# Routing and row scatter of a mixture of experts, moved into the last sections of the transformer before it

## The reference

```python
def _moe(x, rw, rb, w1, b1, w2, b2):          # E = 8 experts, K = 2 chosen, FF = 1024
    xf = x.reshape(T, D)                       # T = 4096, D = 256
    router_weights = jax.nn.softmax(xf @ rw + rb, axis=-1)
    topw, topi = jax.lax.top_k(router_weights, K)
    topw = jax.nn.softmax(topw, axis=-1)
    combine = zeros((T, E)).at[arange(T)[:, None], topi].add(topw)
    h = gelu(einsum('td,edf->etf', xf, w1) + b1[:, None, :])
    eo = einsum('etf,efd->etd', h, w2) + b2[:, None, :]
    return einsum('etd,te->td', eo, combine)
...
x = _layernorm(x + _attn(x, encoder_output, ...), ln2_g, ln2_b)
x = _layernorm(x + _moe(x, router_w, router_b, e_w1, e_b1, e_w2, e_b2), ln3_g, ln3_b)
```

## Time and profile before

| What | Value |
|---|---|
| median of 3 runs | 3463.55 us |
| the profiled execution: its time, its span | 3469.08 us, 3466.9 us |
| PE busy over the span | 2949.5 us (85%) |
| DVE, ACT, POOL busy | 2096.4, 1958.2, 1631.2 us |
| end of the last POOL step of the transformer | 2699.7 us |
| first matmul of the first expert block | 2858.9 us |
| first load of the final section | 3379.3 us |

### The profile page before, as it was taken

The page is one execution under the profiler, slowest core; times in us unless marked ns, Lnnn a source line. Parts: engine busy times, 40 slices in busy tenths (PEclk is TensorE's granted clock), DMA queues, the critical chain, the costliest instruction groups (busy, mean ns, idle before and its releaser), DMA issues. The chain is left out here.

```text
span 3466.9 us, 58062 instructions
## 1 busy us (share of the span) xinstructions
PE 2949.5 (85%) x19009; PEld 1713.3 (49%) x19009; DVE 2096.4 (60%) x4293; ACT 1958.2 (56%) x4164; POOL 1631.2 (47%) x2833
## 2 busy tenths in 40 slices
PE   6889999888989999998988999989888409999990
PEld 3435444543544354445435443544342409999980
DVE  4877796787879678877867796785435200000007
ACT  4675767576756757675766667573534104444431
POOL 4655563673657357546836572664230171111114
PEclk9999999999999999999999999988898559999995
DMA  3004230523144042214213241413330258999974
GB/s 89 16 22 101 58 85 23 123 59 71 53 81 74 28 86 59 55 31 95 54 42 67 57 74 31 86 36 78 58 51 14 79 195 269 326 324 326 324 255 145
DMA packets 309028, 355.41 MB, mean 103 GB/s; under 512 B 33534, under 2 KB 286334, under 8 KB 308656
## 3 DMA queue, kind: packets, MB, share of 16 engines
q1 hardware_dynamic: 300576, 335.27, 37.0%
q0 software_dynamic: 6480, 17.05, 1.3%
q10 hardware_dynamic: 1728, 0.01, 0.0%
HBM read 291.86 MB, written 61.11 MB: 102 GB/s over the span
## 5 line engine op out<-in xcount | busy, mean ns | idle before, releaser
L1254 ACT ACTIVATE probs<-ps,nbias,sc 128x512 f32<-128x512 f32 x1024 | 790.3, 778 | 278.3 <-DVE nbias L1135 219.9
L1001 POOL TENSOR_SCALAR pq<-probs,rstep 128x512 f16<-128x512 f32 x1024 | 713.5, 697 | 251.6 <-PE ps L1368 168.2
L1152 DVE TENSOR_REDUCE m<-ps 128x1 f32<-128x512 f32 (+3 forms) x1024 | 560.6, 582 | 292.8 <-PE ps L1394 150.0
L1132 DVE TENSOR_REDUCE nmax<-ps 128x2 f32<-128x1024 f32 x512 | 620.4, 1212 | 95.9 <-PE ps L1360 95.2
L1391 PE MATMUL ps<-kst,qst 96*128 96x512 bf16 (+3 forms) x1024 | 331.0, 355 | 89.6 <-issue 50.7
L1144 DVE TENSOR_SCALAR big<-ps 128x1024 bf16<-128x1024 f16 x512 | 347.9, 679 | 62.4 <-PE ps L1368 61.0
L1368 PE MATMUL ps<-id,pq 128*128 128x128 f16 x4096 | 331.0, 226 | 47.5 <-DVE big L1144 41.2
L1785 ACT ACTIVATE hT<-moe_ps,e_b 128x128 f32<-128x128 f32 x568 | 208.1, 367 | 280.8 <-PE moe_ps L1728 242.0
L1413 PE MATMUL ps<-qst,kst 108*128 108x512 bf16 (+3 forms) x1024 | 306.1, 353 | 65.0 <-ACT big L1273 29.6
L1368 PEld LDWEIGHTS ps<-id,pq 128*128 128x128 f16 x4096 | 262.0, 101 | 191.4 <-issue 126.2
L1273 ACT ACTIVATE big<-ps 128x512 f32<-128x512 f32 (+3 forms) x640 | 274.1, 480 | 142.0 <-PE ps L1416 96.6
(11 more groups left out here) (202 smaller groups left out, 4609.8 us busy)
## 6 DMA issues: line engine op xcount, KB each, us to landing
e_w<-in_L_xattn_e_w_dram SPq DMA_DIRECT2D x142, 1024.0 KB
wring<-in_L_xattn_ff_w_dram SPq DMA_DIRECT2D x96, 256.0 KB, 2.9
parts<-parts_sb SPq DMA_DIRECT2D x64, 384.0 KB, 3.1
kst<-parts SPq DMA_DIRECT2D x192, 128.0 KB, 4.8
qst<-parts SPq DMA_DIRECT2D x192, 128.0 KB, 5.0
moe_in<-rows_in SPq DMA_DIRECT2D x71, 132.0 KB
rows_in<-zero SPq DMA_DIRECT2D x17, 528.0 KB, 4.1
xn<-in_ctx_dram SPq DMA_DIRECT2D x16, 512.0 KB, 3.9
```

Of the source, the lines that this page charges most:

```text
L1001: nc.gpsimd.tensor_scalar(pq[:, u % 2, h, :], probs[:, u % 2, h, :], rstep[:, u % 2, h:h + 1], HALF_ROUND, ALU.mult, ALU.add).then_inc(SIG ...
L1132: nc.vector.tensor_reduce(nmax[:, n % 2, :], ps[:, a:a + 2, :], AX.X, ALU.max, negate=True).then_inc(SIG["M"], 1)
L1152: nc.vector.tensor_reduce(m32[:, g % 2, t, h:h + 1], bank(("A", B, s, n))[:, 0:width], AX.X, ALU.max, negate=True).then_inc(SIG["am"], 1)
L1254: nc.scalar.activation(probs[:, u % 2, h, :], ps[:, BANKS[("S", B, s, u)][h], :], ACT.Exp, bias=nbias[:, u % 2, h:h + 1], scale=sc[:, s:s ...
```

## The change

The routing and the scatter are done per batch, as steps of the transformer's list: rT and dr (transpose and copy), rL (logits), rl, rx, rm, ry, ri (softmax, two best, weights and choice), rP and rp (places of the rows), and sc (8 indirect DMAs of a batch on POOL). The batches are routed in the order 4, 5, 0, 1, 2, 3, 6, 7. The first may not begin before the exact stage (6, 3). Batches 4 to 7 are still in X, which has 4 places now; batches 0 to 3 are read back from `mid` (step LR on SP) into the places of batches 4 and 5. The weight ring has 6 pieces for 8.

Each expert has a region of 33 blocks in `rows_in`, so a row's place follows from a running count for each expert, and the number of an expert's rows need not be known ahead. A row carries 3 x 8 words behind its 256 features: for each expert where the result goes, its weight, and whether it is the token's first choice. The filling with zero rows is gone: one block of pad rows is written at the start, and after the last routing SP copies it behind the last row of each expert, at the place that the count says (8 copies DRAM to DRAM).

In the experts' part the routing, the loading of `mid` and the scatter are gone. DVE makes the block plan from the counts alone (9 steps for the owners, 8 more for the places of the blocks). SP loads the weights of slot 0 first, then the 4 blocks, then the weights of the slots 1 to 3, and reads a block's place before its load. DVE finishes a part at the end of a block: it multiplies the output and its bias by the weight and adds x for the first choice (4 instructions in place of 2). In the final section DVE adds the two parts in one instruction of 128x1024, adds eps and negates the mean; the shift goes to POOL. A load of the parts of batch c + 4 waits for the output of batch c, where it waited for the sums of batch c.

```diff
-ROW = D + NE
+ROW = D + 3 * NE
 TOKENS = NBATCH * N
+REGION = TOKENS // BLOCK + 1
+NOWHERE = NE * REGION
+ALL_BLOCKS = NOWHERE + 1
+X_DEEP = 4
+ROUTED = (4, 5, 0, 1, 2, 3, 6, 7)
+AGAIN = {0: 0, 1: 1, 2: 0, 3: 1}
+ROUTED_LAST = ROUTED[-1]
...
+    return AGAIN[B] if B in AGAIN else B % X_DEEP
...
-RING = 8
+RING = 6
...
-        step("LX", B, 0, 0, ("ST", B - 3, 5, 0) if B >= 3 else None)
+        step("LX", B, 0, 0, ("ST", B - X_DEEP, 5, 0) if B >= X_DEEP else None)
...
         norm(B, 5)
-        step("ST", B, 5, 0, ("gb", B, 5, NT - 1))
+        last = routed_before(B)
+        if B in AGAIN:
+            step("LR", B, 6, 0, ("ST", B, 5, 0), ("sc", place_taken(B)[-1], 6, 2 * NT - 1))
+        for m in range(KT):
+            step("rT", B, 6, m, ("LR", B, 6, 0) if B in AGAIN else ("gb", B, 5, NT - 1), ROUTING_OPENS if B == ROUTED[0] else ("rL", last, 6, 0))
+            step("dr", B, 6, m, ("rT", B, 6, m))
+        step("rL", B, 6, 0, ("dr", B, 6, KT - 1), last is not None and ("rp", last, 6, 0))
+        step("rl", B, 6, 0, ("rL", B, 6, 0))
+        step("rx", B, 6, 0, ("rl", B, 6, 0))
+        step("rm", B, 6, 0, ("rx", B, 6, 0))
+        step("ry", B, 6, 0, ("rm", B, 6, 0))
+        step("ri", B, 6, 0, ("ry", B, 6, 0))
+        step("rP", B, 6, 0, ("ri", B, 6, 0))
+        step("rp", B, 6, 0, ("rP", B, 6, 0))
+        for n in range(2 * NT):
+            step("sc", B, 6, n, ("rp", B, 6, 0))
+        if B in AGAIN:
+            step("ST", B, 5, 0, ("gb", B, 5, NT - 1))
...
+                if kind == "LR":
+                    sp.wait_ge(s_stored, 16 * B + 16)
+                    sp.wait_ge(s_sc[place_of(B)], 16 * 2 * NT * len(place_taken(B)))
+                    sp.dma_start(X[:, place_of(B), :, 0:D], mid[B].rearrange("(t p) d -> p t d", p=P)).then_inc(s_again[place_of(B)], 16)
...
-                    fill_some_rows()
...
+            after(sp, "rp", ROUTED_LAST, 6)
+            for e in range(NE):
+                if e == 0:
+                    sp.wait_ge(s_zeroed, 16)
+                end = sp.value_load(run_int[0:1, e:e + 1], min_val=0, max_val=NOWHERE * BLOCK - BLOCK)
+                sp.dma_start(every_row[bass.ds(end, BLOCK), :], every_row[NOWHERE * BLOCK:ALL_BLOCKS * BLOCK, :]).then_inc(s_zeroed, 16)
+            sp.wait_ge(s_stored, 16 * len(AGAIN))
+            sp.wait_ge(s_zeroed, 16 * (NE + 1))
+            for place in range(X_DEEP):
+                sp.wait_ge(s_sc[place], 16 * 2 * NT * len([b for b in ROUTED if place_of(b) == place]))
...
+                if kind == "sc":
+                    k, t = n // NT, n % NT
+                    after(pool, "rp", B, s)
+                    nc.gpsimd.indirect_dma_start(rows_in.rearrange("b r d -> (b r) d"),
+                                                 bass.IndirectOffsetOnAxis(ap=slot_of[:, B, k, t:t + 1], axis=0),
+                                                 X[:, place_of(B), t, :], None).then_inc(s_sc[place_of(B)], 16)
...
+                if kind == "ri":
+                    dve.wait_ge(s_route, 6)
+                    for t in range(NT):
+                        last = nc.vector.max_index(idx[:, t, :], top[:, t, :], pr[:, t, :])
+                    then(last, 1)
+                    then(nc.vector.tensor_copy(idf[:, :, :], idx[:, :, 0:2]), 2)
+                    after(dve, "ry", B, s)
...
+                    then(nc.vector.tensor_copy(X[:, place_of(B), :, :].bitcast(U32)[:, :, D:D + NE], goes_to[:, :, :]), 9)
+                    for k in range(2):
+                        last = nc.vector.tensor_tensor(at_pos[:, k, :, :], eq[:, k, :, :], wide(wt[:, k, :]), ALU.mult)
+                    then(last, 10)
+                    then(nc.vector.tensor_tensor(X[:, place_of(B), :, D + NE:D + 2 * NE], at_pos[:, 0, :, :], at_pos[:, 1, :, :], ALU.add), 11)
+                    then(nc.vector.tensor_copy(X[:, place_of(B), :, D + 2 * NE:ROW], eq[:, 0, :, :]), 12)
...
+                if kind == "rp":
+                    after(dve, "rP", B, s)
+                    filled = bank(("rP", B, s, 0))
+                    then(nc.vector.tensor_tensor(pos[:, :, :], filled[:, 0:NT * NE].rearrange("p (t e) -> p t e", e=NE),
+                                                 every_tile(run[:, :]), ALU.add), 1)
+                    then(nc.vector.tensor_tensor(run[:, :], filled[:, NT * NE:(NT + 1) * NE], run[:, :], ALU.add), 2)
+                    for k in range(2):
+                        last = nc.vector.tensor_tensor(at_pos[:, k, :, :], eq[:, k, :, :], pos[:, :, :], ALU.mult)
+                    then(last, 3)
+                    then(nc.vector.tensor_reduce(slot_f[:, :, :], at_pos[:, :, :, :], AX.X, ALU.add), 4)
+                    then(nc.vector.tensor_copy(slot_of[:, B, :, :], slot_f[:, :, :]), 5)
+                    then(nc.vector.tensor_copy(run_int[:, :], run[:, :]), 6)
...
+                if kind == "rL":
+                    after(pe, "dr", B, s, KT - 1)
+                    rest_loaded(pe)
+                    bank_free(pe, e)
+                    for t in range(NT):
+                        for k in range(KT):
+                            last = nc.tensor.matmul(bank(e)[:, t * NE:(t + 1) * NE], rT[:, k, t * P:(t + 1) * P], rw[:, k, :],
+                                                    start=(k == 0), stop=(k == KT - 1))
+                    last.then_inc(SIG["rL"], 1)
+                if kind == "rP":
+                    after(pe, "ri", B, s)
+                    bank_free(pe, e)
+                    flat = chosen[:, :, :].rearrange("p t e -> p (t e)")
+                    nc.tensor.matmul(bank(e)[:, 0:NT * NE], earlier[:, :], flat, start=True, stop=False)
+                    for t in range(1, NT):
+                        nc.tensor.matmul(bank(e)[:, t * NE:NT * NE], ones[:, :], flat[:, 0:(NT - t) * NE], start=False, stop=(t == NT - 1))
+                    for t in range(NT):
+                        last = nc.tensor.matmul(bank(e)[:, NT * NE:(NT + 1) * NE], ones[:, :], flat[:, t * NE:(t + 1) * NE],
+                                                start=(t == 0), stop=(t == NT - 1))
+                    last.then_inc(SIG["rP"], 1)
...
             sp.wait_ge(s_r, OWNERS_READY)
-            for slot in range(WSLOTS):
-                load_weights(slot, slot)
-            sp.wait_ge(s_sc, 16 * 2 * NTILES)
+            load_weights(0, 0)
+            sp.wait_ge(s_r, PLACES_READY)
             for slot in range(WSLOTS):
                 load_block(slot, slot)
+            for slot in range(1, WSLOTS):
+                load_weights(slot, slot)
...
             for c in range(NB):
+                sp.wait_ge(s_y, c + 1)
                 if c + GOTS < NB:
-                    sp.wait_ge(s_add, 2 * NT * (c + 1))
                     load_parts(c + GOTS)
-                sp.wait_ge(s_y, c + 1)
...
-            for c in range(NB):
-                pool.wait_ge(s_x[c], 16)
-                for t in range(c * NT, (c + 1) * NT):
-                    for k in range(2):
-                        nc.gpsimd.indirect_dma_start(rows_in.rearrange("b r d -> (b r) d"),
...
-                    nc.vector.tensor_tensor(yb[:, slot, s, :], ps[:, 2 + 2 * slot + s, 0:D],
-                                            b2[:, bass.ds(e, 1), :].rearrange("p a n -> p (a n)"), ALU.add).then_inc(yd, 1)
+                    done = 3 * (SUB * j + s)
+                    mine = xin[:, ws, s, :]
+                    nc.vector.tensor_copy(words[:, slot, s, :].unsqueeze(2),
+                                          mine.bitcast(U32)[:, D:ROW].rearrange("p (w e) -> p w e", w=3)[:, :, bass.ds(e, 1)]).then_inc(s_words, 1)
+                    nc.vector.tensor_tensor(biased[:, slot, s, :], ps[:, 2 + 2 * slot + s, 0:D],
+                                            b2[:, bass.ds(e, 1), :].rearrange("p a n -> p (a n)"), ALU.add).then_inc(s_words, 1)
+                    dve.wait_ge(s_words, done + 1)
+                    nc.vector.tensor_scalar(residual[:, slot, s, :], mine[:, 0:D], words[:, :, :, :].bitcast(F32)[:, slot, s, 2:3], None, ALU.mult).then_inc(s_words, 1)
+                    dve.wait_ge(s_words, done + 3)
+                    nc.vector.scalar_tensor_tensor(out=yb[:, slot, s, :], in0=biased[:, slot, s, :], scalar=words[:, :, :, :].bitcast(F32)[:, slot, s, 1:2],
+                                                   in1=residual[:, slot, s, :], op0=ALU.mult, op1=ALU.add).then_inc(yd, 1)
 
             for ws in range(WSLOTS):
...
+                    i = c % 2
+                    mine = got[:, c % GOTS, 0, :, :]
                     dve.wait_ge(s_g[c % GOTS], 32 * (c // GOTS) + 32)
-                    for k in range(2):
-                        for t in range(NT):
-                            n = c * NT + t
-                            if k:
-                                dve.wait_ge(s_add, c * 2 * NT + t + 1)
-                            nc.vector.scalar_tensor_tensor(out=tile(c, t), in0=got[:, c % GOTS, k, t, :], scalar=wt[:, k, n:n + 1],
```

(13 more changed lines are left out.)

392 lines of the change are left out of this document (185 added, 207 removed), and 9 rows, old and new, of tables (ON, TAKES).

## The result

The changed kernel takes 3344.65 us, the median of 4 runs (3340.18 to 3349.85), where the kernel before took 3462.54 us beside it. The ratio is 0.966, with a 95% interval of 0.9642 to 0.9679. The forecast was 3340. The profiled execution took 3340.18 us, which is the lowest of the four, while the profiled one before, 3469.08 us, stands above its median. A difference of the two traces is therefore some 10 us larger than that of the medians.

The account below looks back on a forecast made before the run. PE bounds the expert blocks, nearly fills the last transformer sections and idles in a 159.2 us gap; DVE and POOL lead the end. -109.2 - 23.2 + 0.9 + 8 = -123.5 gives 3340 us on the median's scale, range 3312 to 3378.

Parts of the forecast that it names:

- A: Gap between the transformer's last POOL step and the first hidden matmul: 159.2 us shrinks to 50.0, so -109.2.
- B: Final section: period per batch falls from 8.61 to 5.8 us and the last add shortens, -23.2 (-10 to -32).
- C: Expert blocks: PE and DMA set the pace; extra work shows only behind the last block, +0.9 (0 to 2).
- D: Transformer sections taking the moved routing and scatters: mostly hidden, +8 (-10 to +38).
- Routing: In the gap: routing of batch 7, with some 26 small DVE steps, 14 us (11 to 20).
- Pads and scatter: In the gap: batch 7's 8 scatters with 8 pad copies on SP beside them, 13 us (11.3 to 25).
- First weights and block: In the gap: first weights, no longer hidden by the scatter, 7.5 us, then block 0 behind them, 2.3.
- The rule weighed there: Final section: two-input DVE instructions and GpSimd instructions reading SBUF exclude each other; would make the saving 5.6 us smaller.
- The period of 6.6: Final section under full exclusion: add, gain and POOL's 4.2 us in turns per batch; as a rival 3346 us, chance 0.15.
- 6.6 of PE: Section (7, 3), where PE is nearly full: routing of batches 0 and 1 can't hide, 2 x 3.3 us.
- Rival 2: Transformer sections stretch to their bound of +38, as a late rL holds the row maxima: 3370 us, chance 0.15.
- Rival 5: (6, 4) to (7, 4): nothing moved hides, scatters on POOL queue ahead of splits PE needs; 3501 us, chance 0.03.

Follow-up runs that it names:

- e7: The changed kernel with 6 places for the loaded parts in the final section instead of 4: 3343.24 us.
- e8: The changed kernel with the final section's one add of 128x1024 replaced by 8 instructions of 128x256: 3360.85 us.
- e10: The changed kernel with eps added on GpSimd and the shift formed on VectorE in the final section, as before the change: 3358.36 us.
- e9: The changed kernel with constants behind the first weights, bias loads behind stores of split parts, 6 places for loaded parts and 4 for outputs: 3347.83 us.
- e5: The changed kernel with VectorE waiting for the three constants behind its block plan instead of ahead of it: 3344.76 us.
- e12: The kernel before with 4 places for X and a weight ring of 6 pieces together: 3453.94 us.
- e4: The changed kernel with the routing opened only behind batch 7's last gain and bias, all 8 batches routed at the end: 3411.15 us.
- e11: The changed kernel with every scatter of the first 7 batches done twice, the second into a spare DRAM tensor: 3416.63 us.

## Why the prediction was right

The forecast of 3340 lies 4.7 us from the median, and the sum of -123.5 stands against -128.5 in the traces and -118 in the medians. A and B came out, in the main, by the mechanism that was forecast, and C is small as forecast. D did not; its number came out by luck. Point by point:

- **A, the gap**: 50.0 forecast, 52.9 measured (50.8 to 51.0 in e7, e8 and e10, where this part is the same). Routing 14 and 14.2; constants 8.9 and 8.3; plan 3.3 and 3.2 (2738.98 to the end of `owner`, 2742.13); weights' issue 1.0 and 0.8. Pads and scatter 13 and 15.7: the copies are issued 1.38 us apart and land by about 2728.4, and the hand-over between the two parts of the program, some 2.2 us, had been left out. First weights and block 9.8 and 10.8, and the wait that ends last is the block's (`moe_in`), issued 3.1 us behind the weights and landing behind their 2 MB. The routing's 14.2 hides a wait that the forecast did not name: fillers. PE's order puts 31 of them ahead of the place matmul, and DVE stands for it:

```profile
2704.52 8.54 PE L1462 MATMUL ps<-idb 128*128 128x512 bf16 x31
...
2713.35 0.19 DVE L1281 TENSOR_TENSOR pos<-ps,run 128x32 f32<-128x32 f32 x1 [3.14 <-PE ps L1489]
```

The granted clock is 0.79 under them (2704.6 to 2712.9). In e7 it is 1.00 (2713.0 to 2719.6), and the routing takes 12.5 us:

```profile
2712.94 6.85 PE L1462 MATMUL ps<-idb 128*128 128x512 bf16 x31
...
2720.08 0.19 DVE L1281 TENSOR_TENSOR pos<-ps,run 128x32 f32<-128x32 f32 x1 [1.45 <-PE ps L1489]
```

- **B, the final section**: -23.2 and -24.9, period 5.8 and 5.34. One claim in it was wrong, that the loads are not late. With a release by the output, the last adds wait for `got` (0.69 us in the row above); e7 and e9 show two rings, of loads and of outputs, that each bound it.
- **The rule weighed there** shows in single instructions. The deviation on GpSimd takes 1.01 us alone and 2.00 where it begins at 3311.04, with the gain's multiplication on DVE running until 3312.16: it ends 0.9 us behind it, about what exclusion would give. That is what the Trainium skill, "SBUF — State Buffer", section "Who interferes with whom", says of two-input instructions, and this trace agrees. The period of 6.6 that the prediction drew from it did not come. In e9, where no buffer is waited for, one batch reads

```profile
3321.72 1.21 DVE L2008 TENSOR_TENSOR got<-got 128x1024 f32<-128x1024 f32 x1
...
3322.95 2.78 POOL L1840 TENSOR_TENSOR moe_y<-got,bias 128x256 f32<-128x256 f32 x4
...
3325.14 1.67 DVE L2024 TENSOR_TENSOR got<-got,gain 128x1024 f32<-128x1024 f32 x1
3325.69 1.99 POOL L1831 TENSOR_TENSOR moe_rstd<-moe_ve,moe_mh 128x4 f32<-128x4 f32 x1
3326.73 1.21 DVE L2008 TENSOR_TENSOR got<-got 128x1024 f32<-128x1024 f32 x1
```

The adds are 5.01 apart. The bias of 2.78, the gain and the add of 1.21 each make 5.2, less small overlaps, so these three do go in turns; the gain begins before the bias ends and takes 1.67. The deviation is not among the turns: the add runs beside it and takes its usual 1.21. The prediction's 6.6 had counted it (1.02) and a bias of 3.14.
- **C, the blocks**: +0.9 forecast, +1.6 measured, and PE busy for all of 503 us. DVE's extra 53 us lie beside it.
- **D, the sections** is the step that failed in its make-up, though not in its sum: +8 forecast, +1.1 in the first trace, +9 to +12 in e5, e7 and e8, +17.6 in e10. It had priced the work as mostly hidden (6.6 of PE and a little more) and the fourth place as a small help inside a lower bound. In truth places and ring give -17 (e12; 15 by the medians), and the routing with its scatters costs about +26 (e4 against e5, e7, e8), +17 to +34 over all traces. Two errors of some 18 us, of opposite sign, made the number right: that is luck. Where the 6.6 went wrong can be read in part. It put nothing on the stretch from (6, 3) to (6, 4), where DVE is busy for 17 us more than in e4 (136.9 for 119.7) and 7 to 9 us are lost. It counted two batches in (7, 3) and nothing for the three behind them, where fillers were to give way; over those five PE is busy for 12 us more, and 15 to 24 us are lost. And it took the 16 instructions of the logits' row for two batches; they are one (128 for all 8 batches), though batch 7's own then took 1.95 us in the gap, not far from the 1.7.
- **Rival 2**, the stretch to +38, was nearer to what the routing does in most traces than the forecast was. Its mechanism, PE waiting for row maxima held up by the routing, does not show: over 2300 to 2620 PE waits 3.6 us for the row maxima in e5 and 4.8 in e4.
- **Rival 5** named a mechanism, scatters on POOL ahead of what PE waits for, that e11 shows at work on a second dose, with 65 of 71 us exposed. For the first dose it is not shown, and in (6, 4), where the forecast too expected it, that dose costs 1 to 2 us. Its price was wrong too: it charged 7 x 24.1 us, as if a batch's scatter and the next one's routing could not overlap. With all of it bare at the end (e4) the time is 3411, not 3501, and still faster than before. So even the worst placing that was tried left it faster, with the final section's gain in it. The gap of e4 is 142.7 us with all 8 batches in it, where the kernel before needed 159.2; the placing in the sections is worth the rest, 3411 to 3345.
